# Last transformer layer in one Trainium2 kernel: row normalisation moved from VectorE to ScalarE, and the order of a round's blocks and pieces rewritten

## What is computed

```python
ln_out = layernorm(hidden_states, ln1_s, ln1_b)
qkv = ln_out @ w_qkv + b_qkv
ctx = merge_heads(attention(split_heads(q), split_heads(k), split_heads(v), ltor_mask))   # 16 heads of 16
x = hidden_states + ctx @ w_ao + b_ao
ln_out = layernorm(x, ln2_s, ln2_b)
q = ln_out @ w_q + b_q
k, v = jnp.split(encoder_states @ w_kv + b_kv, 2, axis=-1)
ctx = merge_heads(attention(split_heads(q), split_heads(k), split_heads(v), cross_mask))
x = x + ctx @ w_co + b_co
ln_out = layernorm(x, ln3_s, ln3_b)
return x + gelu(ln_out @ w1 + b1) @ w2 + b2
```

## Time and profile before

| | |
|---|---|
| time, median of 3 runs | 1341.6 us (1341.17 to 1344.08) |
| the profiled execution's own time | 1344.38 us |
| its span in the trace | 1342.6 us |
| granted TensorE clock, mean | 0.986 |
| PE busy | 1249.9 us |
| last layer's matmuls | from 1057.6 to 1339.9 us of the span |
| `scores` of rounds 3, 8 and 15 start at | 1109.52, 1170.73, 1241.96 us |

### The profile page before, as it was taken

How to read it: one execution, slowest core, us unless ns; L and a number is a source line. 1 busy time by engine, 2 the same in 40 slices (tenths; PEclk the granted TensorE clock), 3 DMA queues, 4 the chain that set the end, 5 groups by cost and what they waited for, 6 DMA issues and landing times.

```text
span 1342.6 us, 24499 instructions
## 1 busy us (share of the span) xinstructions
PE 1249.9 (93%) x8912; PEld 1021.4 (76%) x8912; DVE 837.7 (62%) x1864; ACT 738.5 (55%) x2000; POOL 568.8 (42%) x583
## 2 busy tenths in 40 slices
PE   6999999999887988999999999999998978988788
PEld 5777777777644557899999889999996646767667
DVE  4666666766549976666666776666675137687521
ACT  4665666566546875545454655455544244666621
POOL 3664555555359963232120413131203146677501
PEclk9999999999998999999999999999999989998999
DMA  6101010100010004111111111120001001000000
GB/s 261 50 27 52 27 52 27 53 27 29 3 65 0 1 1 157 33 48 33 48 32 49 33 48 43 37 72 9 17 1 65 0 0 64 2 1 1 1 12 20
DMA packets 15525, 50.44 MB, mean 38 GB/s; under 512 B 1840, under 2 KB 5296, under 8 KB 14384
## 3 DMA queue, kind: packets, MB, share of 16 engines
q1 hardware_dynamic: 15408, 48.87, 11.0%
HBM read 47.82 MB, written 1.05 MB: 36 GB/s over the span
## 4 chain that ended last, share of the span: by engine, by line
PE 81%; DVE 11%; ACT 4%; issue 2%; POOL 1%; DMA 1%; SPq 0%; DVEq 0%; ACTq 0%
PE pS L1534 13%; PE pT L1562 6%; PE acc L1614 6%; PE acc L326 6%; PE pC L406 4%; PE pT L393 4%; PE pS L376 4%; PE pS L1576 4%; PE pC L1599 4%; PE heads_scores L1355 3%; PE acc L362 3%; PE heads_scores L1344 3%; PE pT L1587 2%; PE heads_scores L2041 2%; DVE stats L1248 2%
## 5 line engine op out<-in xcount | busy, mean ns | idle before, releaser
L1534 PE MATMUL pS<-split_sources,split_pair_weights 128*128 128x512 f32 x768 | 212.0, 411 | 5.8 <-issue 4.3
L722 POOL TENSOR_TENSOR probs<-probs,stats 128x512 f32<-128x512 f32 x128 | 130.5, 1040 | 140.1 <-DVE stats L587 140.1
L528 ACT ACTIVATE probs<-pS,stats 128x256 f32<-128x256 f32 x256 | 117.8, 472 | 102.0 <-DVE stats L582 102.0
L1534 PEld LDWEIGHTS pS<-split_sources,split_pair_weights 128*128 128x128 f32 x768 | 135.9, 190 | 30.7 <-issue 6.6
L1711 ACT ACTIVATE probsT<-pT 128x256 f32<-128x256 f32 x128 | 49.1, 384 | 197.2 <-PE pT L1587 197.2
L1614 PE MATMUL acc<-l_wo_parts,l_ctx_parts 128*128 128x256 f32 x768 | 122.0, 295 | 1.0 <-DVE l_ctx_parts L1783 1.0
L1562 PEld LDWEIGHTS pT<-l_wv_parts,split_sources 128*128 128x128 f32 x756 | 106.9, 188 | 14.2 <-issue 2.2
L1562 PE MATMUL pT<-l_wv_parts,split_sources 128*128 128x256 f32 x756 | 110.6, 281 | 2.1 <-issue 2.1
L1837 POOL TENSOR_TENSOR split_pair_weights<-weights_a,split_pair_weights 128x1024 fp32r<-128x1024 f32 x16 | 38.0, 2378 | 170.1 <-ACT split_pair_weights L1675 170.0
L1614 PEld LDWEIGHTS acc<-l_wo_parts,l_ctx_parts 128*128 128x128 f32 x768 | 99.4, 190 | 1.2 <-DVE l_ctx_parts L1783 1.2
L326 PE MATMUL acc<-split_sources,split_pair_weights 128*128 128x512 f32 x372 | 99.5, 402 | 0.8 <-POOL split_pair_weights L704 0.7
(11 more groups left out here) (253 smaller groups left out, 2899.1 us busy)
## 6 DMA issues: line engine op xcount, KB each, us to landing
weights_a<-in_l_w SPq DMA_DIRECT2D x16, 768.5 KB, 4.3
weights_a<-in_l_w SPq DMA_DIRECT2D x16, 768.0 KB, 5.9
value_bias_rows<-in_l_bv SPq DMA_DIRECT2D x16, 256.0 KB, 4.4
weights_b<-in_l_wo SPq DMA_DIRECT2D x16, 256.0 KB, 2.7
w_fc<-in_l_w SPq DMA_DIRECT2D x4, 1024.0 KB, 5.9
bias_rows<-in_rows SPq DMA_DIRECT2D x1, 1536.0 KB, 13.3
x_residual<-in_x_dbl SPq DMA_DIRECT2D x2, 512.0 KB, 7.0
masked_scores<-in_ctx_dbl SPq DMA_DIRECT2D x2, 512.0 KB, 7.9
```

Source lines behind the costliest of these rows:

```text
L528: a = e.activation(self.E[:, n % 4, h, it, :], self.S[h][:, it, :], ACT.Exp, bias=self.st[:, 1, n % 4, h, it:it + 1], accum_out=self.st[:, ...
L722: e.tensor_tensor(self.E[:, n % 4, h, :, :], self.E[:, n % 4, h, :, :], self.st[:, 3, n % 4, h, :].unsqueeze(2).broadcast_to([P, 2, D]), A ...
L1534: mm = e.matmul(bank[:, :], self.w_qk[i % 2][kw][:, 1 - which, c, h * P:h * P + P], g.split[:, which, ks, c, half * HALF:half * HALF + HAL ...
```

## The change

One function changes engine, and the order changes on all of them:

- `rows` is now an ACT activation with a scale of 1/std and a bias of -mean/std. `rstd_of` on GpSimd makes that bias with two more one-column instructions.
- `FIRST` holds all eight G pieces and begins with T0; G5, G6 and G7 were in steps 0 and 1.
- `STATS` and `ROWS` are one step earlier; `rows_transposes`, `attention_output`, `evacuate_ct` and `add_x` of a round come at step r + 4 and no longer r + 5; `evacuate_c` at r + 3 and no longer r + 4.
- Only a step's first piece stands ahead of `attention_output` on PE, the others behind it.
- The H pieces are spread over steps 15 to 22, O over 19 to 25.
- The blocks of a step stand in another order on ACT, DVE and POOL.

The core of the diff (of the tables a few entries; lines of `...` are left out):

```diff
-    FIRST = ['G0', 'T0', 'G1', 'T1', 'G2', 'K00', 'Q00', 'V00', 'G3', 'K01', 'Q01', 'V01', 'G4']
+    FIRST = ['T0', 'G0', 'K00', 'G1', 'G2', 'V00', 'T1', 'Q00', 'K01', 'G3', 'V01', 'G4', 'G5', 'Q01', 'G6', 'G7']
...
@@ pe
-            if 0 <= t - 5 < self.R:
-                rows_transposes(t - 5)
+            if 0 <= t - 4 < self.R:
+                rows_transposes(t - 4)
             if 0 <= t - 2 < self.R:
                 transposes(t - 2, 0)
-            for p in self.FILL.get(t, []):
+            for p in self.FILL.get(t, [])[:1]:
                 self.pe_piece(e, p)
-            if 0 <= t - 5 < self.R:
-                attention_output(t - 5)
+            if 0 <= t - 4 < self.R:
+                attention_output(t - 4)
+            for p in self.FILL.get(t, [])[1:]:
+                self.pe_piece(e, p)
@@ act
         for p in self.FIRST:
+            if p in ("T0", "T1"):
+                self.rows(e, int(p[1]))
             self.act_piece(e, p)
         for t in range(self.STEPS):
-            if 0 <= t - 4 < self.R:
-                evacuate_c(t - 4)
             if 0 <= t - 2 < self.R:
                 exps(t - 2, 0)
+            for q in self.ROWS.get(t, []):
+                self.rows(e, q)
+            if 0 <= t - 3 < self.R:
+                evacuate_c(t - 3)
+            if 0 <= t - 4 < self.R:
+                evacuate_ct(t - 4)
             if 0 <= t - 2 < self.R:
                 exps(t - 2, 1)
-            if 0 <= t - 5 < self.R:
-                evacuate_ct(t - 5)
@@ rstd_of, rows
+        if q >= 4:
+            e.wait_ge(self.h, 2 * (q - 4) + 2)
...
+        for b in (2 * (q % 4), 2 * (q % 4) + 1):
+            e.tensor_scalar(self.ve[:, b:b + 1], self.mv[:, b, 0:1], self.rs[:, b:b + 1], -1.0, ALU.mult, ALU.mult)\
+                .then_inc(self.rstd, 1)
...
-            e.tensor_scalar(g.hn[:, 2 * (q % 2) + i, :], g.x[:, b, :], self.mv[:, b, 0:1],
-                            self.rs[:, b:b + 1], ALU.subtract, ALU.mult).then_inc(self.h, 1)
+            e.activation(g.hn[:, 2 * (q % 2) + i, :], g.x[:, b, :], ACT.Identity, scale=self.rs[:, b:b + 1],
+                         bias=self.ve[:, b:b + 1]).then_inc(self.h, 1)
@@ dve
                 scale_and_mask(t, 0)
-            for q in self.ROWS.get(t, []):
-                self.rows(e, q)
+            if 0 <= t - 0 < self.R:
+                scale_and_mask(t, 1)
             if 0 <= t - 1 < self.R:
                 maxes(t - 1, 0)
             if 0 <= t - 1 < self.R:
                 maxes(t - 1, 1)
-            if 0 <= t - 0 < self.R:
-                scale_and_mask(t, 1)
-            if 0 <= t - 5 < self.R:
-                add_x(t - 5)
+            if 0 <= t - 4 < self.R:
+                add_x(t - 4)
```

More of the change, by code:

```diff
@@ L1933 @@
     STEPS = R + 10
[L1934 to L1937 removed]
+    FIRST = ['T0', 'G0', 'K00', 'G1', 'G2', 'V00', 'T1', 'Q00', 'K01', 'G3', 'V01', 'G4', 'G5', 'Q01', 'G6', 'G7']
+    FILL = {0: ['U4'], 1: ['U5'], 2: ['U6', 'T2'], 3: ['K02', 'U7', 'Q02'], 4: ['T3', 'V02'], 5: ['K03', 'Q03'], 6: ['T4', 'J00', 'V03'], 7: ['J01', 'Q10'], 8: ['V10', 'T5'], 9: ['J11', 'Q11'], 10: ['V11', 'T6'], 11: ['J10', 'Q12'], 12: ['V12', 'T7'], 13: ['Q13'], 14: ['V13', 'T8'], 15: ['H03', 'H00'], 16: ['H01', 'T9'], 17: ['H02', 'H13'], 18: ['H10', 'H11', 'H12'], 19: ['O0', 'T10', 'O1'], 20: ['H22', 'H20', 'O2', 'T11'], 21: ['H21', 'H23', 'H30'], 22: ['H31', 'H32', 'H33', 'O3'], 25: ['O4', 'O5', 'O6', 'O7']}
+    STATS = {1: [2], 3: [3], 5: [4], 7: [5], 9: [6], 11: [7], 13: [8], 15: [9], 17: [10], 19: [11]}
+    ROWS = {2: [2], 4: [3], 6: [4], 8: [5], 10: [6], 12: [7], 14: [8], 16: [9], 18: [10], 20: [11]}
     def __init__(self, g, cross, m2, weights, masks, w_loaded, masks_ready):
@@ L2402, in dve @@
         add_m2(3)
-        self.rows(e, 0)
         self.statistics(e, 1)
-        self.rows(e, 1)
         for p in self.FIRST:
@@ L2464, in pool @@
         for t in range(self.STEPS):
+            if 0 <= t - 0 < self.R:
+                add_masks(t, 0)
+            for q in self.ROWS.get(t - 2, []):
+                self.add_bias(e, q)
+            if 0 <= t - 0 < self.R:
+                add_masks(t, 1)
             if 0 <= t - 1 < self.R:
                 shift(t - 1, 2)
+            if 0 <= t - 0 < self.R:
+                add_masks(t, 2)
+            for q in self.STATS.get(t, []):
+                self.rstd_of(e, q)
+            if 0 <= t - 0 < self.R:
+                add_masks(t, 3)
             if 0 <= t - 1 < self.R:
                 shift(t - 1, 3)
-            if 0 <= t - 0 < self.R:
-                add_masks(t, 0)
-            if 0 <= t - 0 < self.R:
-                add_masks(t, 1)
-            for q in self.STATS.get(t - 0, []):
-                self.rstd_of(e, q)
-            if 0 <= t - 0 < self.R:
-                add_masks(t, 2)
-            if 0 <= t - 0 < self.R:
-                add_masks(t, 3)
-            for q in self.ROWS.get(t - 1, []):
-                self.add_bias(e, q)
 def store(g, e, ready, base):
```

10 lines of the change are left out of this document (4 added, 6 removed).

## The result

| | median | lowest to highest | n |
|---|---|---|---|
| before | 1341.38 us | 1339.94 to 1344.08 | 4 |
| after | 1301.32 us | 1299.8 to 1304.1 | 4 |

The ratio is 0.9701, with a 95% interval of 0.9677 to 0.9725: 40 us faster, where 27.2 were forecast. The profiled execution of the changed kernel took 1302.4 us, 1.1 above its median, and its span is 1300.6; that of the kernel before took 1344.38, 3.0 above its median of 1341.38. So the two traces lie 42.0 us apart, 1.9 more than the medians.

The account below looks back on a forecast made before the run. PE, busy 93%, was taken as bound, idled by a path through three engines. Gains of 11.4 (B), 1.5 (A), 6.3 (C) and 8 us (Clock) sum to 27.2, so 1341.6 - 27.2 = 1314.4 us; range 1300 to 1331.

Parts of the forecast that it names:

- the forecast's own case: Whole kernel: 1314.4 us likeliest, with 0.3 to 0.9 us idle per middle round; 51 in 100.
- B: `scores` of round 3 to those of round 15: PE idle per round from 1.55 to 0.6 us, 11.4 us gained.
- A: First G to `scores` of round 3: PE idle from 9.0 to 7.5 us, 1.5 us gained.
- C: The tail, from `scores` of round 15: PE idle from 15.8 to 9.5 us, 6.3 us gained.
- T's place: T later in its step, its Q a step further: waits on rows and `hT`, 13.8 us in B, gone.
- The floor: Shortest new round: 8.4 to 8.7 us, from GpSimd's 8.4 and PE's 8.73 us per round.
- B2: Second part of B, `scores` of round 8 to round 15: seven rounds of 10.18 us, PE idle 10.1 us before.
- GpSimd without idle time: Sign in B that the forecast would be wrong; GpSimd was expected at 8.4 us per round, below PE's 8.73.
- `rows` on ScalarE: Rows moved from DVE to ACT: DVE falls to 7.2 us per round, ACT rises to 7.1, neither near PE.
- B1: First part of B, `scores` of round 3 to round 8: PE idle 8.5 us of 61.21 before.
- Clock: Low clock over the four stretches: loss of at most 13.5 us falls to 5.5, 8 us gained.
- the waits go nearly whole: Rival: idle falls to 0.2 us per round in B, 5 in A, 6 in C; 40 us gained, 1302; 18 in 100.

Follow-up runs that it names:

- q_right_behind_t: The changed kernel with Q11, Q12 and Q13 placed directly behind T5, T6 and T7 in the same step, not a step later; 1308.89 us, ratio 0.9752.
- rows_on_scalar_alone: The kernel before in all its orders, but `rows` an ACT activation and its two bias instructions on GpSimd; 1341.0 us, ratio 1.0.
- rows_on_vector: The changed kernel in all its orders, but `rows` back on DVE and without the two bias instructions on GpSimd; 1312.0 us, ratio 0.9771.
- old_start: The changed kernel with the start's G, U, T2 and Q02 pieces nearly at their earlier places, statistics and rows of couple 2 a step later; 1313.92 us.
- gelu_behind_exps: The changed kernel with all H pieces moved to step 18, behind the last exponentials, saving the table loads between them; 1303.22 us, ratio 0.971.

## Why the prediction was right, and where its sizes were off

The direction and the mechanism were right, the size was not: the gain is 40 us for 27.2. The 1301.3 us lie outside the 1307 to 1323 of the forecast's own case, and only 1.3 us inside the stated 1300 to 1331, which had been drawn wide to take in the rivals. That the time falls into the range is in part luck. By the traces the five parts of the 42.0 us are 17.4 in B, 2.6 in A, 7.5 in C, 10.3 by the clock and 4.2 that the sum had no term for; the largest miss is B.

**What bounds the kernel.** Right. The three-engine path was most of the idle time of the rounds (13.9 of 18.6 us by its two waits), and its cut was the largest part of the gain. Both waits behind it vanished; the granted clock of B is 1.00 (0.98 or more foreseen); `scores` 3 to 15 take 104.65 us, though, less than the 112 to 116.

**T's place.** Right, and the term was too small. Idle time in B fell from 18.6 us to 1.2, 0.10 per round for the 0.6 taken: 17.4 us for 11.4. The allowance for new waits on ScalarE (exponentials behind a late copy, `evacuate_ct` behind `rows`) was not needed: the view of PE's waits names neither, only 0.4 us on the copy of the probabilities. The prediction also kept 4.8 us of B's other waits, and these fell to 1.1. q_right_behind_t shows that a Q put back costs 2.2 us for each of three pairs, with the uneven steps in it.

**The floor.** "A floor of the new round is therefore 8.4 to 8.7 us" failed as a number: B2's rounds take 8.19. PE's 8.73 counted matmuls that ran at the low clock or behind a wait before; without these they take 56.59/7 = 8.08. GpSimd's list takes 8.06 and not 8.4: the prediction added up single rows, where the earlier trace rows has 52.74/7 = 7.5 for the list itself, and with its 0.2 for the new instructions 7.8. That GpSimd "becomes the second bound" is right: 0.4 us more of it per step cost 2.5 us in B2, and "GpSimd without idle time" was named as a sign of a wrong forecast, where it now is the sign of a full one, with PE busy 99% beside it.

**`rows` on ScalarE.** Right in size: two take 1.08 us for the 1.02 foreseen, ACT has 6.96 us per round for 7.1, DVE 7.45 for 7.2. The new instructions of `rstd_of` take 0.50 for 0.44. What the prediction didn't say is that this part alone is worth nothing: it gave one sum to all parts of the change, and rows_on_scalar_alone and rows_on_vector show that the move wins 0 without the order and 10.7 us with it, and the order 29.0 without the move.

**A.** Right in size by itself, 2.6 us of idle time for the 1.5 foreseen. The wait of T1 on its rows (1.1 us) is gone as forecast, though T1 stands behind six pieces where it stood behind three, not "six pieces later". But the term stands for less than the start decides: put back, as in old_start, the old places cost 12.6 us in the new orders, by the slow matmuls and by a 3.0 us wait of the first piece behind T2 that falls past the end of A. The prediction had only today's A as its yardstick. How much of the 15.7 us that A and B1 lost is the start's own stays open, since old_start has waits that the kernel before hasn't.

**C.** 15.8 us idle became 8.3, for 9.5 foreseen: 7.5 us gained for 6.3. The waits of steps 16 and 17 for exponentials, 1.65 and 2.44 us, stand where the prediction had 1.5 and 3.3; those of steps 18 and 19 came at 1.08 and 0.90 for 1.1 and 1.2, and the "small ones" of 2.4 us are two more waits of 1.08 for the copied probabilities. The loads between the exponentials cost nothing net, since gelu_behind_exps has the same C without them and without the H work that they make room for.

**Clock.** The bound fell from 13.5 to 3.2 us, 10.3 for the 8 taken. Idle and clock together explain 37.8 of the 42.0 us. The other 4.2 had no term in the prediction, which called all that is neither idle nor low clock "matmul work that the change leaves as it is": they are the overlap of neighbouring matmuls that each of the 27 waits had taken away, 4.4 us by the estimate above.

Taken together, the case that came is the rival "the waits go nearly whole" (1302; 18 in 100), with its B of 0.2 us per round (0.1 measured) and its clock bound of 3 (3.2), while its idle times of 5 in A and 6 in C came at 6.4 and 8.3. The speech against it, that four engines at 7 to 8.7 us in a round of 9 rarely mesh, was the wrong one: at these loads the order written by hand does mesh them.

## What to carry to other kernels

Where PE waits twice on a path over several engines, put the producer a step ahead of its consumer, so that other matmuls cover each handover, before making any operation on the path cheaper: here the operation moved alone only moved the wait to the next engine's queue. Cost a removed wait with the slow matmuls that follow it; here idle time was two thirds of the gain (27.5 of 42.0 us) and slower or less overlapped matmuls the rest. To learn whether an engine has become the bound, give it some half a microsecond more per round and see which stretch grows, by the stretch and not by the total time.

## What the runs showed of the hardware

The normalisation of 128x256 on DVE takes between 400 and 1369 ns (median 808 in rows_on_vector), the same work on ACT 585 to 602. The rows of one line each, of rows_on_vector and of the changed kernel (shortest, median, longest in ns):

```profile
L2330 DVE TENSOR_SCALAR normalised<-x_residual,stats x24: 400/808/1369, 1058.3 to 1274.3; 128x256 f32<-128x256 f32 x24
```

```profile
L2338 ACT ACTIVATE normalised<-x_residual,stats x24: 585/590/602, 1054.0 to 1266.6; 128x256 f32<-128x256 f32 x24
```

The long ones stand beside a GpSimd instruction, and end with it. In the timeline of rows_on_vector two normalisations take 0.72 us where GpSimd is idle, and 1.68 where a GpSimd instruction has just begun:

```profile
1058.28 0.72 DVE L2330 TENSOR_SCALAR normalised<-x_residual,stats 128x256 f32<-128x256 f32 x2
...
1060.96 1.27 POOL L2336 TENSOR_TENSOR x_residual<-x_residual,bias_rows 128x512 f32<-128x512 f32 x1
1061.02 1.68 DVE L2330 TENSOR_SCALAR normalised<-x_residual,stats 128x256 f32<-128x256 f32 x2 [1.14 <-POOL stats L2321]
```

Of the 24 in that trace the six with no GpSimd instruction beside them take 400 to 405 ns. The ten longest, 1349 to 1369 ns, each begin 0.06 to 0.14 us behind the start of a GpSimd instruction and end 0.15 us behind its end. The Trainium skill (SBUF — State Buffer, SBUF: two separate sides) says that GpSimd shares a port pair with DVE, where the DVE instruction is in a two-port mode or has two inputs in SBUF, that one instruction holds the pair to its end while the other is blocked, and that ACT never waits on anyone. The trace agrees with it, by the ends named; no run here took GpSimd's work away to prove it. The rule of the Trainium skill (ScalarE: Activation LUTs, Rules for kernel authors) that multiply and add belong on VectorE, for which it gives DVE's speed in bf16, did not hold here for fp32: beside a busy GpSimd ACT was the cheaper engine, 590 ns for 808 in the median, while DVE without GpSimd beside it took 400 to 405.

The exponentials start 0.01 us after the end of a table load (1233.55 against 1232.26 + 1.28) in the changed kernel, and 0.02 before; and the load itself starts 0.02 us behind the copy of `hT` ahead of it (1231.22 + 1.02). The 1.38 us drain that the Trainium skill (ScalarE: Activation LUTs, What ACT_TABLE_LOAD costs) adds to a load shows on neither side of it.

At the start, where gaps of 1.4 to 1.5 us follow one another, the same sixteen matmuls of a U piece took 5.14 us once and 3.69 the next time. PE's timeline of the changed kernel:

```profile
1086.70 5.14 PE L1355 MATMUL heads_scores<-w_fc,hidden_b 128*128 128x256 f32 x16 [1.53 <-DVE masked_scores L2378]
...
1095.06 3.69 PE L1355 MATMUL heads_scores<-w_fc,hidden_b 128*128 128x256 f32 x16 [1.43 <-DVE probs L2378]
```

The windows of these two pieces have the granted clock, 0.71 in the first and 1.00 in the second; at 0.71 the low level's bound is (1 - 0.71) x 5.14 = 1.5 us, and the two differ by 1.45:

```profile
1086.70:1091.84 5.14, 5.14 (x16) 4.00 (x16) 0.99 (x1) 0.00 (x0) 4.93 (x4) 0.71 0.01 3
1095.06:1098.75 3.69, 3.69 (x16) 2.92 (x16) 3.23 (x3) 1.55 (x6) 2.80 (x3) 1.00 0.00 0
```

The gaps ahead of both are nearly the same, so a gap's length alone doesn't say whether the low level follows.
